# Expert stage of a graph and mixture-of-experts layer: seven blocks of gathers ahead, the two adds of a block in flight together, four result buffers, weight rows in 2 KB pieces

## The reference

```python
logits = xt @ Wr + br
probs = jax.nn.softmax(logits, axis=-1)
top_p, top_idx = jax.lax.top_k(probs, TOP_K)
weights = top_p / top_p.sum(axis=-1, keepdims=True)
...
xe = xn[None, :, :] * ln_g[:, None, :] + ln_b[:, None, :]
h = jax.nn.gelu(jnp.einsum('end,edh->enh', xe, W1) + b1[:, None, :], approximate=False)
y = jnp.einsum('enh,ehd->end', h, W2) + b2[:, None, :]
...
sel = jnp.take_along_axis(y_tok, top_idx[:, :, None], axis=1)
out = (weights[:, :, None] * sel).sum(axis=1)
```

## Time and profile before

| what | value |
|---|---|
| median of 3 runs | 2677.9 us (2674.82 to 2684.92) |
| the profiled execution: time | 2665.86 us |
| the profiled execution: span | 2664.0 us |
| first up-matmul to last down-matmul of the experts | 1896.6 to 2647.7 us |
| PE busy over the whole span | 64% |
| DMA engines' mean busy share in the expert stage | about 66% |

### The profile page before, as it was taken

The page is one execution under the profiler, slowest core; times in us unless marked ns, Lnnn a source line. Parts: engine busy times, 40 slices in busy tenths (PEclk is TensorE's granted clock), DMA queues, the critical chain, the costliest instruction groups (busy, mean ns, idle before and its releaser), DMA issues.

```text
span 2664.0 us, 33981 instructions
## 1 busy us (share of the span) xinstructions
PE 1711.4 (64%) x10955; PEld 1312.6 (49%) x10955; DVE 1248.1 (47%) x3231; ACT 726.1 (27%) x1605; POOL 1685.8 (63%) x1107
## 2 busy tenths in 40 slices
PE   2443445556666666666666634775877878777876
PEld 1211233334444444444554524664866767666765
DVE  2334334334444444444665542558645555545453
ACT  1011123333223222321211102443433333333332
POOL 3766777778888888888888888880233333333332
PEclk9656657777778777887888857986999989989998
DMA  9998887777555555555555547885367666666664
GB/s 274 202 164 115 142 139 125 125 110 103 71 71 68 70 71 71 71 71 71 69 69 71 71 34 138 179 159 184 98 203 220 206 205 204 207 195 214 194 215 113
DMA packets 373460, 358.28 MB, mean 134 GB/s; under 512 B 43317, under 2 KB 340738, under 8 KB 358692
## 3 DMA queue, kind: packets, MB, share of 16 engines
q0 software_dynamic: 146880, 92.09, 33.1%
q1 hardware_dynamic: 226404, 264.03, 32.8%
HBM read 247.03 MB, written 108.96 MB: 134 GB/s over the span
## 4 chain that ended last, share of the span: by engine, by line
DMA 52%; POOL 21%; issue 13%; PE 9%; DVE 2%; SPq 1%; POOLq 1%; ACT 0%; DVEq 0%; ACTq 0%
DMA node_table<-edge_sums,row_i 30%; POOL node_table L1418 19%; DMA result<-mixw,slot_tok 12%; DMA state<-L_gnn_z_in,in_deg 6%; PE bank L678 4%; DMA edge_rows<-xn_rows,slot_tok 4%; PE bank L664 2%; POOL edge_rows L1451 1%; PE bank L632 1%; PE bank L634 1%; PE bank L650 1%; SPq L1488 1%; POOL result L1463 0%; DMA node_numbers<-id_rows 0%; POOLq L1418 0%
## 5 line engine op out<-in xcount | busy, mean ns | idle before, releaser
L1418 POOL DMA_INDIRECT node_table<-edge_sums,row_i x782 | 1244.1, 1591 | 363.8 <-DMA node_table<-edge_sums,row_i 173.8
L446 PE MATMUL bank<-edge_rows,same_node 128*128 128x130 f32 x1564 | 314.8, 353 | 578.5 <-issue 372.7
L446 PEld LDWEIGHTS bank<-edge_rows,same_node 128*128 128x128 f32 x1564 | 270.5, 251 | 729.6 <-issue 695.3
L1463 POOL DMA_INDIRECT result<-mixw,slot_tok x105 | 168.7, 1607 | 454.6 <-DMA result<-mixw,slot_tok 312.7
L1229 ACT COPY edge_sums<-bank 128x390 f32<-128x390 f32 (+1 forms) x261 | 126.4, 484 | 1199.3 <-DMA node_table<-edge_sums,row_i 1138.9
L1372 ACT ACTIVATE mixw<-bank,m_r 128x256 f32<-128x256 f32 (+1 forms) x456 | 242.5, 549 | 494.7 <-PE bank L664 333.9
L678 PE MATMUL bank<-big 128*128 128x256 f16 x2520 | 315.7, 290 | 1.0 <-issue 1.0
L664 PE MATMUL bank<-edge_rows,big 128*128 128x256 f16 (+1 forms) x2736 | 286.8, 265 | 5.4 <-DMA big<-w_parts 5.4
L678 PEld LDWEIGHTS bank<-big 128*128 128x128 f16 x2520 | 260.4, 104 | 44.4 <-issue 1.3
L664 PEld LDWEIGHTS bank<-edge_rows,big 128*128 128x128 f16 x2736 | 250.6, 98 | 34.4 <-DMA big<-w_parts 7.4
L546 PE MATMUL bank<-mixw,big 128*128 128x512 f32 x392 | 264.8, 812 | 4.0 <-ACT big L1282 4.0
(11 more groups left out here) (255 smaller groups left out, 2382.2 us busy)
## 6 DMA issues: line engine op xcount, KB each, us to landing
big<-w_parts SPq DMA_DIRECT2D x114, 1024.0 KB, 5.8
edge_rows<-edge_attr SPq DMA_DIRECT2D x130, 384.0 KB, 3.9
big<-L_ffn_W SPq DMA_DIRECT2D x128, 128.0 KB, 3.5
w_parts<-big SPq DMA_DIRECT2D x64, 256.0 KB, 3.9
node_table<-zeros SPq DMA_DIRECT2D x20, 645.0 KB, 8.7
node_table<-edge_sums,row_i POOLq DMA_INDIRECT x782, 3.6
mixw<-node_table SPq DMA_DIRECT2D x96, 129.0 KB, 3.7
b2r<-L_ffn_b SPq DMA_DIRECT2D x57, 128.0 KB
```

The source lines that it names most:

```text
L446: ins = e.matmul(ps_sum[:, i * XW:(i + 1) * XW], S[:, g % SRING, i * P:(i + 1) * P], X[:, c // LOAD % XRING, c % LOAD, :], start=True, sto ...
L1418: e.indirect_dma_start(table[t], bass.IndirectOffsetOnAxis(ap=row_i[:, g % ORING, i:i + 1], axis=0), O[:, g % ORING, i, 0:RW], None, compu ...
L1463: e.indirect_dma_start(y_rows, bass.IndirectOffsetOnAxis(ap=slot_tok[:, tile:tile + 1], axis=0), yo[:, j % 2, s, :], None, compute_op=ALU. ...
```

## The change

- Gathers: the ring `xg` moves from the edges' area to `state`, which nobody needs after its rows are stored to the result, and holds eight blocks where it held four. The first gather therefore also waits for those stores (`y_store`). The loads of the two tiles of one block count on one semaphore.
- POOL's order: at block j first the adds of block j, and then the gathers of block j+7 (before: first the gathers of block j+3, and then the adds of block j).
- Adds: only the first add of a block waits for the adds before it; the second follows at once. Both tiles of a block belong to one expert, so they hold different nodes. For the empty slots the spare rows are doubled (odd tiles use rows 128 further on), with which `xn_rows` and the result have 6538 rows in place of 6400, zeroed by six transfers of 96 rows where there were four of 75. In the routing one tiny DVE operation is added.
- Results: `yo` has four blocks in place of two, and the wait for a free one looks back four blocks.
- Weights: each of the two weight transfers is issued with rows cut in pieces of 1024 elements (2 KB) where there was one of 4096 (8 KB).

```diff
-    XG = 4
+    XG = 8
     edge_mem = X.rearrange("p a b c -> p (a b c)")
-    xg = edge_mem[:, 0:XG * 2 * DIM].bitcast(F16).rearrange("p (r s i k n) -> p r s i k n", r=XG, s=2, i=2, k=KC)
-    xT = edge_mem[:, XG * 2 * DIM:(XG + 2) * 2 * DIM].bitcast(F16).rearrange("p (r i k n) -> p r i k n", r=2, i=2, k=KC)
+    xg = state.rearrange("p t n -> p (t n)")[:, 0:XG * 2 * DIM].bitcast(F16).rearrange(
+        "p (r s i k n) -> p r s i k n", r=XG, s=2, i=2, k=KC)
+    xT = edge_mem[:, 0:2 * 2 * DIM].bitcast(F16).rearrange("p (r i k n) -> p r i k n", r=2, i=2, k=KC)
     at[0] = 0
-    yo = part(2 * 2 * DIM).rearrange("p (r h n) -> p r h n", r=2, h=2)
+    YO = 4
+    yo = part(YO * 2 * DIM).rearrange("p (r h n) -> p r h n", r=YO, h=2)
...
@@ vector_route
-        then(e.tensor_scalar(spare1, spare, 1.0, None, ALU.add))
+        then(e.tensor_scalar(spare_col, iota_i[:, 0:STILES], 1, P.bit_length() - 1, ALU.bitwise_and, ALU.logical_shift_left))
+        then(e.tensor_scalar(spare_row, spare_col, spare, 1.0, ALU.add, ALU.add))
...
@@ vector_down
-            if s == 0 and j >= 2:
-                e.wait_ge(row_added, 16 * tiles_before[j - 1])
+            if s == 0 and j >= YO:
+                e.wait_ge(row_added, 16 * tiles_before[j - YO + 1])
...
@@ pool_gather
             e.wait_ge(routed, ROUTE_SLOTS)
-            e.wait_ge(pad_zero, 64)
+            e.wait_ge(pad_zero, 96)
+            e.wait_ge(y_store, 16 * YSTORES)
             rows_stored(e)
...
@@ pool_add
-        if j == 0:
-            e.wait_ge(y_store, 16 * YSTORES)
         for s, tile in enumerate(blocks[j][1]):
             o = tiles_before[j] + s
             e.wait_ge(y_weighed, 2 * o + 2)
-            if o:
+            if s == 0 and j:
                 e.wait_ge(row_added, 16 * o)
...
@@ pool_program
         for j in range(BLOCKS):
+            pool_add(e, j)
             pool_gather(e, j + XG - 1)
-            pool_add(e, j)
         e.wait_ge(row_added, 16 * tiles_before[BLOCKS])
...
@@ load_block, at W1 and the same at W2
-                    w_parts[0][bass.ds(which, 1)].rearrange("o p n -> p (o n)")).then_inc(w1_load[r], 16)
+                    w_parts[0][bass.ds(which, 1)].rearrange("o p n -> p (o n)"), max_dma_last_dim=2048).then_inc(w1_load[r], 16)
```

More of the change, by code:

```diff
@@ L35 @@
 ROWS = (TILES + 1) * P
+PAD = 96
+YROWS = NODES + 3 * PAD
+assert 2 * P <= 3 * PAD
 ZERO = 645
@@ L127, in build_layer @@
     table = [nc.dram_tensor(f"node_table{i}", (ROWS, RW), F32, kind="Internal").ap() for i in range(TABLES)]
-    xn_rows = nc.dram_tensor("xn_rows", (ROWS, 2 * DIM), F16, kind="Internal").ap()
+    xn_rows = nc.dram_tensor("xn_rows", (YROWS, 2 * DIM), F16, kind="Internal").ap()
     y_rows = out
@@ L292, in build_layer @@
     valid = part(1)
-    spare1 = part(1)
+    spare_row = part(STILES)
+    spare_col = part(STILES).bitcast(I32)
     MG, MR = 7, 8
@@ L339, in build_layer, with gathers_of @@
     THREE = ((0, 0), (0, 1), (1, 0))
-    def gathers_of(j, h):
-        return sum(h < len(blocks[i][1]) for i in range(j % XG, j + 1, XG))
+    def gathers_of(j):
+        return sum(len(blocks[i][1]) for i in range(j % XG, j + 1, XG))
     def slots_of(j):
@@ L382, in build_layer @@
     w1_load, w2_load, meta_load = sems("w1_load", 2), sems("w2_load", 2), sems("meta_load", NM)
-    gathered, row_added = sems("gathered", 2 * XG), sem("row_added")
+    gathered, row_added = sems("gathered", XG), sem("row_added")
     x_turned, x_kept, up_done, gelu_done = sem("x_turned"), sem("x_kept"), sem("up_done"), sem("gelu_done")
@@ L643, in tensor_turn @@
             e.wait_ge(x_kept, j)
-        for h in range(len(blocks[j][1])):
-            e.wait_ge(gathered[j % XG * 2 + h], 16 * gathers_of(j, h))
+        e.wait_ge(gathered[j % XG], 16 * gathers_of(j))
         for i in range(2):
@@ L1142, in vector_route @@
         then(e.tensor_scalar(empty, ps_tok, 0.5, None, ALU.is_lt))
-        then(e.tensor_scalar(empty, empty, spare1, -1.0, ALU.mult, ALU.add))
-        e.tensor_tensor(slot_tok, empty, ps_tok, ALU.add).then_inc(routed, 1)
+        then(e.tensor_tensor(empty, empty, spare_row, ALU.mult))
+        e.scalar_tensor_tensor(slot_tok, empty, -1.0, ps_tok, ALU.add, ALU.add).then_inc(routed, 1)
         then(e.tensor_scalar(slot_f, ps_tok, 1.0, None, ALU.max))
@@ L1173, in vector_down @@
     def vector_down(e, j):
-        r, n = j % 2, j % NM
+        r, n = j % YO, j % NM
         if j == 0:
@@ L1451, in pool_gather @@
             e.indirect_dma_start(xg[:, j % XG, h].rearrange("p i k n -> p (i k n)"), None, xn_rows,
-                                 bass.IndirectOffsetOnAxis(ap=slot_tok[:, s:s + 1], axis=0), bounds_check=ROWS - 1,
-                                 oob_is_err=True).then_inc(gathered[j % XG * 2 + h], 16)
+                                 bass.IndirectOffsetOnAxis(ap=slot_tok[:, s:s + 1], axis=0), bounds_check=YROWS - 1,
+                                 oob_is_err=True).then_inc(gathered[j % XG], 16)
     def pool_add(e, j):
-        if j == 0:
-            e.wait_ge(y_store, 16 * YSTORES)
         for s, tile in enumerate(blocks[j][1]):
@@ L1460, in pool_add @@
             e.wait_ge(y_weighed, 2 * o + 2)
-            if o:
+            if s == 0 and j:
                 e.wait_ge(row_added, 16 * o)
-            e.indirect_dma_start(y_rows, bass.IndirectOffsetOnAxis(ap=slot_tok[:, tile:tile + 1], axis=0), yo[:, j % 2, s, :], None,
-                                 compute_op=ALU.add, bounds_check=ROWS - 1, oob_is_err=True).then_inc(row_added, 16)
+            e.indirect_dma_start(y_rows, bass.IndirectOffsetOnAxis(ap=slot_tok[:, tile:tile + 1], axis=0), yo[:, j % YO, s, :], None,
+                                 compute_op=ALU.add, bounds_check=YROWS - 1, oob_is_err=True).then_inc(row_added, 16)
     def pool_program(e):
@@ L1492, in zero_pads @@
         for rows in (xn_rows, y_rows):
-            for a in range(NODES, ROWS, 75):
-                e.dma_start(rows[a:a + 75, :], zeros[0:75, 0:DIM] if rows is y_rows else
-                            zeros[0:75, 0:DIM].bitcast(F16)).then_inc(pad_zero, 16)
+            for a in range(NODES, YROWS, PAD):
+                e.dma_start(rows[a:a + PAD, :], zeros[0:PAD, 0:DIM] if rows is y_rows else
+                            zeros[0:PAD, 0:DIM].bitcast(F16)).then_inc(pad_zero, 16)
     def store_numbers(e, c):
@@ L1700, in load_block @@
         e.dma_start(W2r[:, r].rearrange("p i h n -> p (i h n)"),
-                    w_parts[1][bass.ds(which, 1)].rearrange("o p n -> p (o n)")).then_inc(w2_load[r], 16)
+                    w_parts[1][bass.ds(which, 1)].rearrange("o p n -> p (o n)"), max_dma_last_dim=2048).then_inc(w2_load[r], 16)
     def sync_program(e):
@@ L1755 @@
         args.append(nc.dram_tensor(name, a.shape, mybir.dt.from_np(a.dtype), kind="ExternalInput").ap())
-    result = nc.dram_tensor("result", (ROWS, DIM), F32, kind="ExternalOutput").ap()
+    result = nc.dram_tensor("result", (YROWS, DIM), F32, kind="ExternalOutput").ap()
     build_layer(nc, *args, result)
```

## The result

The changed kernel takes **2521.4 us** (median of 4 runs, 2520.0 to 2525.0) against 2676.4 us of the kernel before (4 runs): a ratio of 0.9425, with a 95% interval of 0.9396 to 0.9453. The prediction was 2530 us, with 2495 to 2600 as its range.

What follows compares the result with a forecast made beforehand. The in-order chain of adds paced the gathers, and these PE; -126.5 gather waits, -43 slow clock, -5.4, -1.0, -6.1 tail, +34 weight stalls, +0.2 gave -148 us, so 2518 us, plus 12.0 to the median: 2530 us, range 2495 to 2600.

Steps and rivals of the forecast that it cites:

- What goes: Expert stage: PE's gather waits of 126.5 us vanish, as does slow clock of 43 us.
- The chain after: POOL's adds in the expert stage: pair to pair 6.4 to 10.7 us, under PE's 10.93 us.
- Rival B: Expert stage: adds still pace at 12.9 us a pair, about 2575 us in all; chance 0.09.
- The stage without stalls: PE's expert stage with nothing late, plus 1.9 us for two slow first ups: 575.1 us.
- Weights: PE in the expert stage waits for W1 twice around each single: 18 stalls of 1.9 us, 34 us.
- 2 KB pieces: Weight transfers in the expert stage: +0.5 us for each, so W1, behind W2, lands 1.0 us later.
- the fit: Cost of each piece on a DMA engine, from edge-row and weight transfers: 0.021 us.
- Rival A: Expert stage: small transfers get in ahead of W1's last pieces, weights late at every block, 2617 us; chance 0.12.
- the rule on turns: DMA engines alternate queues by packet, some 9 to 17 descriptors, 64 at most; 32 pieces might become several packets.
- The tail: From the end of the last down to the end of the span: 10.3 us in place of 16.4.
- The sum: Whole kernel: 1896.55 + 575.1 + 0.2 + 34 + 10.3 = 2516 us of span, then 2530 us as median.
- the forecast's own range: Whole kernel if weights stall only around singles: 2500 to 2560 us; this case's chance 0.74.

Runs made afterwards that it cites:

- e1_unchained: The kernel before, with only the first add of a block waiting for earlier adds and with doubled spare rows: ratio 0.9390 to the kernel before.
- e2_lead: The kernel before, with eight blocks of gathers in the state's area and adds ahead of gathers, every add still chained: ratio 0.9987 to the kernel before.
- e12_tinyweights: The kernel before, with weight transfers from block 2 on cut to 128 bytes a partition, adds still chained: one run, 2481.9 us.
- e6_w1first: The changed kernel with W1 of block j issued ahead of W2 of block j-1 in SP's queue: 2480.4 us, ratio 0.9322 to the kernel before.
- e7_rows512: The changed kernel with weight rows in pieces of 512 B in place of 2 KB: ratio 0.9541 to the kernel before.
- e5_chained: The changed kernel with every add again waiting for the one before it: ratio 0.9829 to the kernel before.

## Why the prediction was right

- **What bounds the kernel** was read rightly: the in-order chain of adds paced the gathers and through them PE. e1_unchained and e2_lead show it from both sides, and e12_tinyweights shows the part that the prediction used as its upper end, 8.8 us beside the weights against 4.5 alone.
- **What goes**: 126.5 us of gather waits and 43 us of slow clock. Measured: only the first two turns still wait, and the clock is 0.99. Right, but for the slow matmuls behind two weight stalls. But the text gave the credit to seven blocks of lead and the unchained adds together; the lead had no part in it.
- **The chain after**: 6.4 to 10.7 us a pair, under PE's 10.93. In the rows above it takes 10.85 us, PE's pace, and is no longer the limit. The second add comes 2.54 us after the first, not 1.9, because it waits for DVE. Rival B did not happen.
- **The stage without stalls**, 575.1 us: e6_w1first took 576.6 us to the start of its last matmul. Right to 0.3%.
- **Weights**: 34 us as 18 stalls of 1.9. Measured 23.3 us in 15 waits, 0.2 to 2.9 us each. This is the term that was mis-sized, and by its count, "twice for each single". The first up after a single's own up waits at 8 of the 9 singles, 0.7 to 2.9 us and 2.0 in the mean, close to the 1.9. The second one, behind the single's down, waits at 3 only (3.7 us together). In the rows above its W1 is issued at the end of the down of 1959.07 (at 1965.65), and the stall of 2.76 us at 1967.23 lies between that issue and the up that needs it (1975.55), so it is given 2.76 us more and is not late. The other 4 waits, 3.5 us together, come at a single's own up or between pairs, where none was forecast; W1's landing was 11.6 us at the most, where I had at most 9.7 + 1.0.
- **2 KB pieces**: put at +1.0 us on W1's landing, 18 us in all. Measured against 8 KB rows 12.6 us of stage, and by e7_rows512 the price for a piece is lower than the fit's 0.021 us: W2's median landing is 6.6 us with 128 pieces an engine, and was 5.2 with 8 in the kernel before, that is 0.012 us a piece. With 2 KB pieces W2's median landing was 5.6 us in e5_chained, 0.4 more than with 8 KB, where the fit said 0.5, and W1's in the changed kernel 8.8, 0.7 more and not 1.0. Right in sign, somewhat too dear.
- **Rival A and the rule on turns.** The Trainium skill (DMA: Bandwidth & Descriptors, Queues, rings and completion order) lets an engine change queues between packets. If smaller pieces had made the turns finer, an add beside the weights would land sooner. From the second add of a pair to the next block's first one it takes 8.37 us in e1_unchained with 8 KB rows and 8.41 us in the changed kernel with 2 KB rows (medians over the 47 such rows of POOL's timeline); both include waits for DVE, so this says only that no gain is seen. Rival A had W1 ready 12.2 us after a down at every block; it is ready 1.15 + 8.8 = 10.0 us after it in the median (the issues lie 1.15 us apart now), inside PE's 10.93. A did not happen; how the engines take turns inside a transfer stays open.
- **The tail**: 10.3 us predicted, 9.6 measured.
- **The sum**: from the first up to the end of the last down 609.1 us predicted (575.1 + 34), 607.0 measured (1906.07 to 2513.1). Part of the closeness is luck. The waits for weights were put 10.7 us too high; all the rest, 607.0 - 23.3 = 583.7 us, was put 8.6 us too low. In this rest are the slow matmuls behind two stalls, which the forecast had at nothing (an up of 7.08 us for 5.40, and one at 2475.32 much like it), and the idle of 1.0 us before the last down, which the forecast let go and which the changed kernel still has. The profiled execution's stage began 9.3 us later than assumed, in stages that the change barely touches, and the spread of that start over the runs is wider than this. Against it stand the 12.0 us that the forecast added from profiled execution to median: the changed kernel's median lies 3.6 us below its profiled execution. That is luck too.
- **A slip in the range**: half of 18 stalls of 0.9 us is 8 us above no stall at all, not 4, so the lower end of the forecast's own range should have been 2504 us. The result lies above either.

The difference of the medians is 155 us, 148 were forecast.

## What to carry to other kernels

When serial transfers pace a kernel, look at what moves beside them before shortening anything else: here a chained add cost 8.8 us next to megabyte transfers and 4.6 without them, and taking one wait in two away ended PE's waits for gathers. A longer lead does nothing while the queue that issues it is stuck behind such a chain (ratio 0.9987), and may be worth 14 (by the ratios) to 26 us (by one profile each) once the weights come in time; so test the parts of a change one by one and again after the next limit is gone. The limit after this one was the order of two weight loads in one queue: issue first what is needed first.

## What the runs showed of the hardware that was not expected

- Cutting 8 KB rows into 512 B pieces, sixteen times as many, moved a 1 MB weight transfer's median landing only from 5.2 us (W2 in the kernel before) to 6.6, yet the stage grew from 594.1 to 642.6 us: W1, which is issued right behind W2, landed 10.6 us after its issue, where it was 8.1 in the kernel before.
- How long PE stood still did not alone decide whether it ran slowly afterwards. After waits of 2.76 and 2.87 us the up took its 5.4 us, after one of 2.61 us it took 7.08, with a granted clock of 0.77 from 2284 to 2291 us. Over the stage the clock was still 0.99, where waits like the one of 6.64 us before had brought it to 0.92.
